# Convolution passes of a graph network on one core: one TensorE signal per four steps, two sets of comparisons, a ring of 14 slots

## The reference, cut to what matters

```
# two convolutions (norm is split into a factor before and one after the sum)
h = x @ W
msg = h[row] * norm[:, None]
out = jax.ops.segment_sum(msg, col, num_segments=n)
# last layer
messages = jnp.take(x, src, axis=0) @ W
aggr_out = jax.ops.segment_sum(messages, tgt, num_segments=x.shape[0])
out = aggr_out + x @ W_self
```

## Time and profile before

| | us |
|---|---|
| three runs without a profile | 10517.32, 10520.3, 10532.23 |
| median | 10520.3 |
| the profiled execution's own time | 10607.1 |
| its span, first to last instruction | 10605.0 |
| convolutions and linear layer in it, first gather to the end | 7111.4 to 10605.0 |
| TensorE's mean granted clock, share of full speed | 0.716 |

### The profile page before, as it was taken

One profiled execution on the slowest core, in us unless ns is written; L12 is line 12 of the kernel. 1 busy time (PEld: TensorE's weight loads), 2 busy tenths in 40 slices (PEclk: granted clock), 3 DMA queues, 4 the chain that ended last, 5 costly groups with the idle time before them and its releaser, 6 DMA issues.

```text
span 10605.0 us, 107124 instructions
## 1 busy us (share of the span) xinstructions
PE 5675.4 (54%) x23750; PEld 3922.0 (37%) x23751; DVE 3028.2 (29%) x7366; ACT 949.0 (9%) x1767; POOL 6216.3 (59%) x6738
## 2 busy tenths in 40 slices
PE   3566637566775667656675666653334333333334
PEld 2333437333443334433343333333333333333234
DVE  3444577212221122312222122331122112231222
ACT  1111100111111111101111111110000000000000
POOL 3655536565555655466554655546666666656665
PEclk7566659777887788878788778875566556665666
DMA  5777755332323323233332323221111111111111
GB/s 167 218 219 218 203 139 155 90 88 82 85 75 86 87 82 85 79 85 87 83 83 75 88 81 81 77 59 45 47 49 48 46 46 49 48 46 46 47 49 47
DMA packets 796948, 945.08 MB, mean 89 GB/s; under 512 B 269045, under 2 KB 530448, under 8 KB 796302
## 3 DMA queue, kind: packets, MB, share of 16 engines
q0 software_dynamic: 213408, 463.35, 16.4%
q1 hardware_dynamic: 474970, 390.60, 13.2%
q10 hardware_dynamic: 108436, 89.99, 2.6%
HBM read 797.55 MB, written 152.25 MB: 90 GB/s over the span
## 4 chain that ended last, share of the span: by engine, by line
another core or an unknown queue 44%; PE 18%; issue 13%; DVE 9%; DVEq 3%; POOL 0%; SPq 0%; ACT 0%; DMA 0%; ACTq 0%; POOLq 0%
PE ps_big L1119 8%; PE ps_seg L1126 5%; DVE onehots L1715 2%; DVE sums L1746 2%; DVEq L453 1%; PE ps_seg L1197 1%; PE ps_big L1197 1%; PE ps_big L1063 1%; PE ps_t L1038 1%; DVE gate L1894 1%; DVE h_res L1898 0%; DVE group_stats L1783 0%; PE ps_seg L1063 0%; PE ps_big L987 0%
## 5 line engine op out<-in xcount | busy, mean ns | idle before, releaser
L871 POOL DMA_INDIRECT rows<-node_rows,idx_all x5488 | 5209.8, 949 | 3470.5 <-SPq L713 1590.0
L1119 PE MATMUL ps_big<-rows,ident 128*128 (+1 forms) x1960 | 1221.8, 709 | 1386.0 <-DVE onehots L1715 1249.5
L1746 DVE TENSOR_TENSOR sums<-sums,ps_seg 128x128 f32 x1342 | 385.5, 287 | 5141.3 <-remote 3368.8
L1126 PEld LDWEIGHTS ps_seg<-onehots 128*128 128x128 f32 x7840 | 1206.0, 223 | 899.0 <-issue 735.5
L1126 PE MATMUL ps_seg<-onehots 128*128 128x128 f32 x7840 | 1236.4, 309 | 260.6 <-issue 168.0
L1715 DVE SCALAR_TENSOR_TENSOR onehots<-ps_mm,away 128x512 f32<-128x512 f32 x1975 | 1349.3, 684 | 21.4 <-issue 13.8
L1197 PE MATMUL ps_seg<-rows,onehots 128*128 (+1 forms) x2952 | 613.8, 372 | 1235.4 <-DVE onehots L1715 595.8
L1119 PE MATMUL ps_big<-q_res,ident 128*128 (+1 forms) x1960 | 1153.9, 674 | 150.9 <-issue 123.0
L1119 PEld LDWEIGHTS ps_big<-rows,ident 128*128 128x128 f32 x1960 | 412.0, 224 | 2036.2 <-DVE onehots L1715 1461.7
L871 POOL DMA_INDIRECT sums<-kv_rows,idx_all x784 | 743.4, 948 | 548.2 <-SPq L711 281.2
L1197 PEld LDWEIGHTS ps_seg<-rows,onehots 128*128 128x128 f32 x2952 | 536.7, 272 | 1301.7 <-DVE onehots L1715 619.0
(11 more groups left out here) (215 smaller groups left out, 2974.4 us busy)
## 6 DMA issues: line engine op xcount, KB each, us to landing
q_res<-gates_by_edge SPq DMA_DIRECT2D x784, 256.0 KB
rows<-node_rows,idx_all POOLq DMA_INDIRECT x5488
rows<-dst_padded SPq DMA_DIRECT2D x196, 256.0 KB
value_rows_by_edge<-sums SPq DMA_DIRECT2D x196, 256.0 KB
gates_by_edge<-gate ACTq DMA_DIRECT2D x196, 256.0 KB
rows<-value_rows_by_edge SPq DMA_DIRECT2D x196, 256.0 KB, 3.5
node_rows<-h_res ACTq DMA_DIRECT2D x49, 448.0 KB
sums<-kv_rows,idx_all POOLq DMA_INDIRECT x784
```

The costliest lines, as they stand in the source:

```text
L871: pool.indirect_dma_start(target[:, r, j, :], None, table, bass.IndirectOffsetOnAxis(ap=idx_all[:, c * J + j:c * J + j + 1], axis=0), elem ...
L1119: last = nc.tensor.matmul(ps_big[u][:, :], ident[:, :], chunk_words(source, slot, 0, CHUNK), start=n == 0, stop=n == 1)
L1126: last = nc.tensor.matmul(ps_seg[u][:, 0:D], onehots[:, u, j, :], msg[:, u, j, 0:D], start=j == 0, stop=j == J - 1)
L1746: V.tensor_tensor(mine, mine, seg_four[(n - 1) % depth][:, 0:D], ALU.add).then_inc(agg_added, 1)
```

## The change

In the three last passes:

- The ring has 14 slots (WIDE). It lies over `rows` and the end of `q_res` before it, which these passes don't use; both are now parts of one tensor, `stock`. GpSimd has a gather loop of its own for it (gather_wide).
- TensorE puts the four sums of a turn side by side into one bank, ps_seg[half], and signals segsum_ready only after the fourth. Two banks take turns. The 244 steps are counted from step 0; the extra first step is gone.
- There are two sets of four comparisons, `onehots` and `marks_odd` (in the space of `score`). VectorE waits for a turn's signal, makes its four adds, then the four comparisons for the turn two later.
- SyncE rounds the step at which a slot is free up to a whole turn.
- A group is now transposed at the end of a turn (conv_turn, with a wait for node_finished), and multiplied at the end of the next.
- Tables of slots for the wide ring and words by turn are made and loaded in addition (wide_d, row_turns, sum_turns: eleven loads on SyncE's queue once the message layer has added its last gates).
- The semaphores gates_landed and values_landed become one set, slot_loaded.

The diff's core:

```diff
-                def sum_rows(slot, u, marked):
+                def sum_rows(slot, n, half, marked):
+                    marks = onehots if half == 0 else marks_odd
                     pe.wait_ge(onehot_ready, marked)
                     for j in range(J):
-                        last = nc.tensor.matmul(seg_four[u][:, 0:D], onehots[:, u, j, :], chunk_words(rows, slot, j * D, D),
-                                                start=j == 0, stop=j == J - 1)
-                    last.then_inc(segsum_ready, 1)
+                        last = nc.tensor.matmul(ps_seg[half][:, n * D:n * D + D], marks[:, n, j, :],
+                                                chunk_words(wide_rows, slot, j * D, D), start=j == 0, stop=j == J - 1)
+                    if n == UNROLL - 1:
+                        last.then_inc(segsum_ready, 1)
...
+                        if i_conv == 2 and n == 1 and not is_first(i):
                             with pe.If(words[10] != 0), clamped(pe, words[11:12], 0, GROUPS - 1) as group:
+                                conv_self(group[0])
+                    if not is_first(i):
+                        with pe.If(words[10] != 0), clamped(pe, words[11:12], 0, GROUPS - 1) as group:
+                            conv_sum(group[0])
+                        with pe.If(words[8] != 0), clamped(pe, words[9:10], 0, GROUPS - 1) as group:
+                            conv_turn(group[0])
...
                 def conv_turn(g):
+                    wait_alone(pe, "pe", node_finished, n_conv * GROUPS + g + 1)
                     turn_group(n_conv, g, 2 if i_conv < 2 else 4)
...
+            def conv_pass(k, start, finish, halves):
...
+                for n in range(2 * UNROLL):
+                    mark_step(n * J, n % UNROLL, (onehots, marks_odd)[n // UNROLL])
...
+                def steps_of(i, words, half, ahead=True):
+                    upto = [dve.compute_val(i * UNROLL + base + n) for n in range(1, UNROLL + 2)]
+                    dve.wait_ge(segsum_ready, dve.compute_val(i + (turn_no(k) + 1)))
+                    for n in range(UNROLL):
+                        mine = sums[:, ds(up_to(words[n], (WINDOWS - 1) * AGGW), D)]
+                        dve.wait_ge(agg_added, upto[n])
+                        V.tensor_tensor(mine, mine, ps_seg[half][:, n * D:n * D + D], ALU.add).then_inc(agg_added, 1)
+                    for n in range(UNROLL if ahead else 0):
+                        mark_step(i * (UNROLL * J) + (n + 2 * UNROLL) * J, n, (onehots, marks_odd)[half])
...
+            def conv_slots(k):
+                begun = turn_no(k)
+                wait_alone(sp, "sp", group_stored, (k - 1) * (16 * GROUPS))
+                wait_alone(sp, "sp", segsum_ready, begun)
+                for r in range(WIDE):
+                    sp.sem_inc(slot_free, 1)
+                def free_turn(turn):
+                    freed, regs = load_free(turn * RING - WIDE, RING)
+                    for r in range(RING):
+                        sp.wait_ge(segsum_ready, ((freed[r] + (UNROLL - 1)) >> (UNROLL.bit_length() - 1)) + begun)\
+                            .then_inc(slot_free, 1)
...
+            def gather_wide(k, table, part_):
+                uses = (k - CONV_PASS) * (CHUNKS // WIDE)
+                landed_before = (0, (LAYERS + 1) * (CHUNKS // RING) * (16 * J))
+                def tell_rows(c):
+                    pool.wait_ge(wide_landed[c % WIDE], landed_before[c % WIDE // RING] + (uses + c // WIDE + 1) * (16 * J)).then_inc(rows_ready, 1)
+                for c in range(CHUNKS):
+                    wait_alone(pool, "pool", slot_free, (k - 1) * CHUNKS + c + 1)
+                    for j in range(J):
+                        pool.indirect_dma_start(
+                            wide_ring[:, c % WIDE, j, :], None, table,
...
+                        if j == J - 2 and c > 0:
+                            tell_rows(c - 1)
+                tell_rows(CHUNKS - 1)
```

172 lines of the change are left out of this document (127 added, 45 removed).

## The result

The changed kernel takes 10574.07 us (median of six runs, 10554.56 to 10579.02), the kernel before, beside it on the same chip, 10513.77 us (10499.05 to 10532.23). The ratio is 1.0055, with a 95% interval of 1.0042 to 1.0067: 0.55% slower. The forecast was 10190 us, range 10050 to 10380, with 0.10 for slower. It was wrong in sign.

A forecast was written before the change was run, and what follows sets the result against it. It took GpSimd's slot waits on late TensorE signals, and what stands between passes, to bound the convolutions. -345 + 9 + 4 = -332 us took the profiled 10607.1 to 10275, less 86.8 to the median: 10190 us, range 10050 to 10380.

The forecast's parts named there:

- Signals: TensorE in the convolutions: 61 signals a pass in place of 245, so it falls behind only 0.8 to 5.0 us a turn.
- Ring: GpSimd's gather slots: 14 hold 70.0 us, a signal may be 45.5 us late; stops of 7 to 53 us a pass.
- 3 x (45 - 160.0) = -345 us: GpSimd's slot waits in three convolution passes: 45 us a pass left of 160.0, bounds 7 and 113.
- Only the ring counts: Convolutions: signals are about 30 us late however few, only extra slots help; 101 us of stops a pass, 10356 us, chance 0.20.
- The change doesn't do what it says: Convolutions: freeing by whole turns eats what the added slots give, slot waits stay; 10533 us, chance 0.06.
- Slower, by the groups: Convolutions' 21 node groups: TensorE stands on held signals or hands groups on late, 30 us each; 10683 us, chance 0.09.
- Ends of passes: After each convolution pass's last gather, TensorE's last steps follow VectorE's marks again: +3 us a pass, +9 in all, up to +30.
- Loads and tables: SyncE's eleven extra loads, covered before the convolutions, plus small VectorE operations at the start and one store: +4 us with margins.

The follow-up runs named there:

- the pauses: Changed kernel plus a GpSimd memset of 0.95 us ahead of every second chunk of gathers, in the convolutions: 10673.24 us, ratio 1.0069 to the kernel before.
- the ring alone: Kernel before with its TensorE and VectorE code kept and only 14 slots added: 10671.48 us, ratio 1.0066 (upper level); 8715.24 us, 1.0009 (lower level).
- the half-matmul pass: Changed kernel's second convolution pass with two of four matmuls per step, other passes altered otherwise; whole run 10631.35 us, kernel before 10611.38.

## Why the prediction was wrong

**The step that failed** is in "Signals" and "Ring": "while gathers flow, a signal of TensorE gets through about every 17 us", so that one signal a turn "nearly keeps up", and "a signal may be 45.5 us late before GpSimd stops. First late by 16.9, then 0.8 more each turn". It took lateness for a toll per signal. In before every step had one signal, so its rows couldn't tell a toll on the signal from one on the step's matmuls. In the trace after, the first turn's matmuls end at 7086.97 and its adds come 15.0 us later, the second turn's end at 7106.97 and its adds come at 7164.31, 57.3 us later, when the first stop had lasted 11 us. A quarter of the signals didn't come sooner: 84 of 183 turns had their adds over 15 us late, and 87 had them in a stop, though stops are 13% of the passes. A long flow lets a step through each 17 to 22 us, with a signal of its own or without; a turn of four then takes 68 to 88 us of flow, by this estimate, against 16.1 us of gathers, and falls behind by over 50 us where the prediction had 0.8 to 5.0. With one signal per step on the same ring the stops were 461.3 us against 454.8. The term 3 x (45 - 160.0) = -345 us measured -25 us (454.8 - 480.1).

**The size of the ring.** The working let a flow last as long as the ring: 14 slots, 70 us of gathers. Only a pass's first flow has that length and more (72 gathers, 89.6 us). Afterwards a flow lasts for as many slots as the last stop set free, 5.5 in the mean, whatever the ring holds, because GpSimd starts again at the first free slot and the hold is back with it. So the stops of a pass are not the price of a buffer that is too short. They are 147 to 169 us in every kernel that does all of its work on the upper level, with 7 or 14 slots, signals by step or by turn, one bank for a turn or four, and 173 with the pauses counted in. A buffer evens out who is late; it doesn't give TensorE the time without gathers that it needs here.

**The rule that was set aside.** The prediction quoted the Trainium skill, "Perfetto Trace Analysis", section on the Tensor engine instruction: a matmul's end is estimated, and by that rule the matmuls might really end late and signalling less would buy nothing. It was set aside because four adds came within 2.4 us after a stop. (The last of the four was not "long there": its matmuls run at 7165.21 to 7167.28, 8.6 us before its add.) Signalling less did buy nothing. But the traces bear the rule's reason out in part only: an end is estimated, a start isn't, and the starts crawl in the changed kernel and not in before, in the ring alone (41 late starts, 57 us, with 475.2 us of stops) or in the half-matmul pass, where adds are late all the same. Whether a matmul's end or its signal is what is late in these no trace here can tell.

**Rivals.** "Only the ring counts" had most of the mechanism, lateness that doesn't go by the number of signals, but priced it by the ring's length (stops of 101 us a pass; 152 measured). "The change doesn't do what it says", 10533 us at 0.06, came nearest in time. Its mechanism, whole turns eating the ring's gain, is not what happened, since undoing them left the stops. "Slower, by the groups" had the sign and not the cause: TensorE's waits at the transposes in the first pass fell from 33.0 us to:

```profile
PE ps_t L1105 <- DVE nodes L2079: 13.9, 6, 3.9
```

**Ends of passes.** Forecast +9 us, bound +30; measured +26 before the next pass's first gather and +13 behind the last, 39 in all and past the bound. The mechanism was the one named: with up to 14 chunks landed and not summed, TensorE goes through whole turns after the last gather and must wait for VectorE's marks once more. TensorE's timeline from 9349 us:

```profile
9351.81 5.25 PE L1278 MATMUL ps_seg<-stock,onehots 128*128 x31 [1.74 <-issue]
9356.90 3.82 PE L1278 MATMUL ps_seg<-stock,score 128*128 x32
9370.37 6.58 PE L1278 MATMUL ps_seg<-stock,onehots 128*128 x32 [9.65 <-DVE onehots L1816]
```

Three turns, with 9.65 us for marks. It was mis-sized because the forecast had the stops gone and TensorE up to date at a pass's end. On the lower level, where it is, the gaps with all 14 slots in use (one signal per step: 21.2, 28.4, 23.2 us) and of before (20.1, 27.5, 19.8) agree within about 3.5 us.

**Loads and tables.** +4 forecast, 5 to 7 us measured, and at the start of the kernel; the eleven loads ahead of the convolutions are hidden, as worked out: the wait before the first pass's first gather is 55.0 us, before 55.13.

**What isn't placed.** Of the 60 us, 6 are the first gather and 19.5 the convolutions by the first pair of profiles. The rest lies between a profile of before that was 93 us over its median and one of after that wasn't. A rival that the expectations name, that the changed kernel loses in the message layers too, stays open on the upper level: from first gather to the convolutions three kernels with the wide ring take 6977 to 6983 us beside before's 6967, and a fourth 6964. On the lower level nothing is lost there (5542 to 5554 us, before 5544 to 5555). The ring alone, where the account closes, has 50 of its 76 us behind the passes; it makes the ring's backlog the likely bulk of the changed kernel's loss too, which seven slots on the upper level in all three passes would have shown. No such run fell on the upper level, nor did a further profile of before. No version is shown to beat the kernel before; seven slots with the changed TensorE and VectorE code (1155.4 us for its one pass) would be the one to try, without the 5 to 7 us at the start.

## What to carry to other kernels

Before a buffer is made deeper, ask whether the consumer is late now and then or held for as long as the producer runs: sum the stops per pass, and if the flows after the first are shorter than the buffer, more slots may, as here, only move work behind the last transfer. A signal that comes late doesn't say that signals are what is slow: where each step has one, the toll may be on the step's work. A kernel without the producer, or with pauses in it, tells whether the producer holds the consumer. And a wait that bounds a kernel should be found again in a second profile before its removal is priced: here it was 480 us or 0.9 us, with the same code.

## What the runs showed of the hardware

- Two levels of one kernel: 10504 to 10611 us and 8706 to 8721 us for the kernel before, over eight series (four on each level), with one chip at 8706 in one series and at 10611 in another. Within a series the runs of one kernel lie within 0.5%. The difference, some 1850 us, is nearly all waits for slots in all eight passes of gathers (in the changed kernel L854 454.8, L735 1058.1, L733 280.6 us; with seven slots on the lower level 0.6, 6.7 and 2.4); without gathers in the convolutions the upper level costs nothing there (1002 against 1001 us). What puts an execution on a level isn't known from these runs.
- On the upper level, 46 us after a pass's gathers begin and mostly 9 to 16 us after those of a later flow, the changed kernel's matmul instructions start 2.1 to 2.8 us apart in place of 0.1 to 0.4, SyncE's register operations of 33 ns take up to 1.4 us, and its adds begin 0.14 to 57.5 us after the last matmul of their turn (over 15 us in 84 of 183; 0.14 us in the median on the lower level). Gathers themselves keep their 0.94 us. In the kernel before and in the ring alone the starts within a step don't crawl, but a step gets through a long flow about every 17 to 22 us there too. After the first pass's first flow the crawl ended 11 us after the last gather.
- All traces are of recorded executions. The three runs of the kernel before that are listed as without a profile took 10517 to 10532 us, so they were on the upper level too; whether recording has a part in the hold can't be told from these runs.
